# Eight weight transposes moved behind the batches' matrices in the first part of a two-layer attention kernel

## The reference

```
x = x + xattn0(layernorm(x), ctx)          # softmax attention, 16 heads of 32, with biases and temperatures
x = x + ffn0(layernorm(x))                 # relu(quant_linear(x, w1, b1)) -> quant_linear(., w2, b2)
x = x + xattn1(layernorm(x), ctx)          # scores without softmax, then layernorm(q + o)
x = x + tanh(layernormed x through three 512x512 matrices + bias)
# quant_linear rounds the weights per output row: s = max|w| / 127, q = clip(round(w / s), -128, 127)
```

## Time and profile before

| | us |
|---|---|
| median of 3 runs | 2006.84 (2006.36 to 2008.04) |
| the profiled execution's own time | 2011.76 |
| its span | 2010.0 |
| TensorE busy in the span | 1871.1 (93%) |
| VectorE, ScalarE, GpSimd busy | 1583.9, 1232.9, 952.4 |

### The profile page before, as it was taken

One profiled execution on the slowest core, in us unless ns is written; L12 is line 12 of the kernel. 1 busy time (PEld: TensorE's weight loads), 2 busy tenths in 40 slices (PEclk: granted clock), 3 DMA queues, 4 the chain that ended last, 5 costly groups with the idle time before them and its releaser, 6 DMA issues. The chain is left out here.

```text
span 2010.0 us, 30847 instructions
## 1 busy us (share of the span) xinstructions
PE 1871.1 (93%) x9191; PEld 1364.4 (68%) x9274; DVE 1583.9 (79%) x3612; ACT 1232.9 (61%) x3387; POOL 952.4 (47%) x1053
## 2 busy tenths in 40 slices
PE   6698789999999999999986999988999999999997
PEld 5576577877777778777863444446767767767775
DVE  6846578888887888888765888887888888888884
ACT  3434588888787878888862333235655555555543
POOL 2210355555555555555551000025666666666664
PEclk9799799999999999999998999999999999999999
DMA  8346101222223212321117999825445445444310
GB/s 276 122 136 220 48 32 58 71 77 64 64 69 81 64 61 63 78 64 43 42 50 274 391 353 363 317 108 205 147 157 185 156 159 186 159 159 159 139 53 38
DMA packets 124680, 276.03 MB, mean 137 GB/s; under 512 B 41056, under 2 KB 51296, under 8 KB 106208
## 3 DMA queue, kind: packets, MB, share of 16 engines
q1 hardware_dynamic: 121680, 272.69, 39.6%
q10 hardware_dynamic: 2832, 1.32, 0.3%
HBM read 165.95 MB, written 108.00 MB: 136 GB/s over the span
## 5 line engine op out<-in xcount | busy, mean ns | idle before, releaser
L1095 POOL TENSOR_TENSOR a_pr<-a_pr,a_rcp 128x512 f32<-128x512 f32 x256 | 266.5, 1041 | 348.5 <-DVE a_rcp L948 348.5
L871 ACT ACTIVATE a_pr<-a_s,a_nmax 128x128 f32<-128x128 f32 x1024 | 361.6, 368 | 64.4 <-DVE a_nmax L941 62.3
L1322 PE MATMUL f_pair<-f_room,w 128*128 128x512 bf16 x999 | 226.2, 383 | 11.8 <-DVE hmax L1549 9.2
L941 DVE TENSOR_REDUCE a_nmax<-a_s 128x4 f32<-128x512 f32 x256 | 175.6, 686 | 56.7 <-PE a_s L60 52.9
L871 ACT ACTIVATION_READ_ACCUMULATOR a_pr<-a_s,a_nmax 128x1 f32 x1024 | 211.0, 206 | 0.0
L1549 DVE CUSTOM_DVE_ANT_0 f_hf<-f_pair,nb,sh 128x512 f32<-128x512 f32 x248 | 175.0, 748 | 39.7 <-PE f_pair L1322 25.6
L956 DVE TENSOR_TENSOR a_pTl<-a_pt,a_pTh 128x512 fp32r<-128x512 f32 x256 | 175.3, 685 | 37.4 <-ACT a_pTh L880 37.4
L1769 POOL TENSOR_TENSOR f_ring<-f_ring,f_room 128x512 f32<-128x512 f32 x64 | 82.1, 1282 | 256.0 <-DVE f_room L1710 256.0
L1322 PEld LDWEIGHTS f_pair<-f_room,w 128*128 128x128 bf16 x1024 | 99.6, 99 | 126.7 <-DVE hmax L1549 9.7
L880 ACT ACTIVATE a_pTh<-a_pt 128x512 fp32r<-128x512 f32 x256 | 156.0, 609 | 29.9 <-PE a_pt L784 29.9
L784 PE MATMUL a_pt<-ident,a_pr 128*128 128x128 f32 x1024 | 157.2, 276 | 16.4 <-POOL a_pr L1095 8.7
(11 more groups left out here) (398 smaller groups left out, 5245.4 us busy)
## 6 DMA issues: line engine op xcount, KB each, us to landing
hidden<-f_hf SPq DMA_DIRECT2D x58, 1024.0 KB, 7.1
f_hf<-hidden SPq DMA_DIRECT2D x58, 1024.0 KB, 5.2
xb<-x SPq DMA_DIRECT2D x16, 1024.0 KB, 5.4
a_xr<-x SPq DMA_DIRECT2D x64, 256.0 KB, 3.6
x<-a_xr SPq DMA_DIRECT2D x64, 256.0 KB, 2.1
f_ring<-x SPq DMA_DIRECT2D x64, 256.0 KB, 4.8
out<-f_ring SPq DMA_DIRECT2D x64, 256.0 KB, 4.5
f_room<-x SPq DMA_DIRECT2D x15, 1024.0 KB, 9.7
```

The lines of the kernel that those rows point to most:

```text
L871: last = e.activation(pr[:, t, j, :], s_bank[t][:, j * P:j * P + P], ACT.Exp, bias=nmax[kk % 2][:, t, j:j + 1], accum_out=sums[kk % 2][:, ...
L941: e.tensor_reduce(nmax[kk % 2][:, t, :], s_bank[t][:].rearrange("p (j n) -> p j n", j=4), AX, ALU.max, negate=True).then_inc(*e_max)
L1095: e.tensor_tensor(p, p, rcp[kk % 2][:, t, :].unsqueeze(2).to_broadcast([P, 4, KEYS]), ALU.mult).then_inc(*e_pn)
L1322: last = e.matmul(h_bank[(PAIRS * u + i) % 3][:, q, :], w1[:, k, f * P:f * P + P], xT[u % 2][:, k, :], start=k == 0, stop=k == KC - 1)
```

## The change

- The transposes of pieces 0 to 3 leave their places behind `V`, `k1`, `v1` and `bd`. Piece 0 stands behind `bd` of batch 0; the others stand behind `mb` of the batches by the tuple `TURNS`, 1 then 2 then 3 and 4 then 5 and 6; piece 7 stands between `wc` 1 and `wc` 2, with the `row` product.
- VectorE quantises piece 0 behind the third weight, and the others by `PARTS`: 1, then 2 and 3, then 4 and 5, then 6, each ahead of that batch's `mb`; piece 7 behind the four `t`. There are three `qb` tiles.
- The transposes of a piece are two lots of eight into whole banks of 1024 columns, and ScalarE makes two copies instead of four.
- The raw loads come in another order. The eight first chunks are split pairwise (ctx, then weight), and the first product follows them pair by pair. The four bias rows move from ScalarE's queue to SyncE's; the three small vectors are issued by ScalarE behind its eight chunks.
- The centring of Wo1 stands between the second and third evacuation of `k1`; `v1` is evacuated in two pairs around the split of Wq1; in batch 3 the split of A2 stands behind the copies of `m`.

```diff
-        order = [plain("ctxT"), plain("WkT0"), w1_rows(0), plain("WvT0"), plain("WkT1"), w1_rows(1), plain("WvT1"),
-                 w1_rows(2), plain("WoT1"), plain("Wq1"), w1_rows(3), w2_rows(0), w2_rows(1), w2_rows(2), plain("A1T"),
+        order = [plain("ctxT"), plain("WkT0"), plain("WvT0"), plain("WkT1"), w1_rows(0), plain("WvT1"), w1_rows(1),
+                 plain("WoT1"), plain("Wq1"), w1_rows(2), w1_rows(3), w2_rows(0), w2_rows(1), w2_rows(2), plain("A1T"),
                  plain("A2"), w2_rows(3), plain("WT"), plain("WqT0"), plain("WoT0"), x_rows[0], x_rows[1]]
+        TURNS, PARTS = ((1,), (2,), (3, 4), (5, 6)), ((1,), (2, 3), (4, 5), (6,))
...
# TensorE
+                for h in range(2):
+                    e_turned.wait_ge(e, 2 * (q - 1) + h)
+                    for m in (2 * h, 2 * h + 1):
+                        for j in range(4):
+                            at = (m % 2) * D + j * P
+                            last = e.transpose(bankb[h][:, at:at + P], part, identb[:])
...
                 product(place["mb"][b], ...)
+                for q in TURNS[b]:
+                    turn(q)
...
# ScalarE
-            with nc.allow_non_contiguous_dma(reason="few small vectors"):
-                for o, i in small:
-                    e.dma_start(o, i).then_inc(*e_small)
-            chunks(0, ctxT)
-            chunks(1, slot[0])
+            chunks()
+            with nc.allow_non_contiguous_dma(reason="few small vectors"):
+                for o, i in small:
+                    e.dma_start(o, i).then_inc(*e_small)
...
             blocks(0)
-            turned(0, 3)
+            turned(0)
...
# VectorE
             weight(1)
+            quantise(0)
             biased("V", 0, 4)
-            quantise(0, 1)
             weight(2)
-            biased("k1", 1, 8)
-            quantise(0, 2)
+            biased("k1", 1, 8, (0, 1))
             centre(W_LOAD[W_CENTRED])
+            biased("k1", 1, 8, (2, 3))
             weight(3)
+            biased("v1", 2, 12, (0, 1))
             weight(4)
-            biased("v1", 2, 12)
-            quantise(0, 3)
+            biased("v1", 2, 12, (2, 3))
             blocks(0)
-            quantise(1, 0)
...
+                for q in PARTS[b]:
+                    quantise(q)
...
# SyncE
+            load(2)
+            load(3)
+            for i in range(3):
+                bias_row(i)
+            load(4)
+            load(5)
             for c in range(KC):
                 send_k(c)
             load(6)
+            load(7)
             for b in range(NB):
                 send_v(b)
+            bias_row(3)
+            for i in (8, 9, 10, 11):
                 load(i)
             send_m(0)
+            load(12)
+            send_m(1)
+            load(13)
+            load(14)
+            send_m(2)
+            load(15)
+            send_w2(0)
+            load(16)
+            load(17)
+            send_m(3)
+            send_w2(1)
+            send_w2(2)
+            for i in (18, 19, 20, 21):
                 load(i)
+            send_w2(3)
```

More of the change, by code:

```diff
@@ L90, in prepare @@
         bqf = sb("bqf", [P, KC, P])
-        rows = sb("rows", [P, 4, D])
-        qb = [sb(f"qb{i}", [P, 4, D], BF16) for i in range(2)]
+        rows = sb("rows", [P, 3, D])
+        qb = [sb(f"qb{i}", [P, 4, D], BF16) for i in range(3)]
         wst = [sb(f"wst{i}", [P, 4, D], BF16) for i in range(2)]
@@ L136, in prepare @@
         e_first, e_raw = [[ev(f"first{i}{q}", 16) for q in range(KC)] for i in range(2)], [ev(f"raw{i}", 16) for i in range(ring)]
-        e_small = ev("small", 16)
+        e_small, e_rows = ev("small", 16), ev("rows", 16)
         e_zero, e_ident, e_identb, e_ones, e_half, e_diag, e_zeroed = (
@@ L156, in prepare @@
                  (cols[:, 3, :], A["L1_xattn_wq_b"].rearrange("(c p) -> p c", p=P))]
-        for i, n in enumerate(("L0_xattn_bv", "L1_xattn_wk_b", "L1_xattn_wv_b", "L1_xattn_wo_b")):
-            small.append((rows[:, i, :], A[n].rearrange("(a n) -> a n", a=1).to_broadcast([P, D])))
+        ROWS = ("L0_xattn_bv", "L1_xattn_wk_b", "L1_xattn_wv_b", "L1_xattn_wo_b")
+        TURNS, PARTS = ((1,), (2,), (3, 4), (5, 6)), ((1,), (2, 3), (4, 5), (6,))
         block = ctx.enter_context(nc.Block())
@@ L173, in product, with turn @@
                 last.then_inc(*e_prod)
-            def turn(which, i):
-                u = i % 2
-                q = 4 * which + i
+            def turn(q):
+                which, i = divmod(q, 4)
                 e_quant.wait_ge(e, q)
                 e_identb.wait_ge(e, 0)
[L180 to L185, removed]
+                for h in range(2):
+                    e_turned.wait_ge(e, 2 * (q - 1) + h)
+                    for m in (2 * h, 2 * h + 1):
+                        for j in range(4):
+                            part = qb[q % 3][:, m, cut(j)] if which else qb[q % 3][:, j, cut(m)]
+                            at = (m % 2) * D + j * P
+                            last = e.transpose(bankb[h][:, at:at + P], part, identb[:])
                     last.then_inc(*e_turn)
@@ L241, in _ @@
                                         for q in range(KC)])
[L242 to L249, removed]
             e_wlo.wait_ge(e, 7)
@@ L252, in _ @@
             for i in range(KC):
+                if i == 2:
+                    turn(7)
+                    p = place["row"][0]
+                    e_ones.wait_ge(e, 0)
+                    e_dg.wait_ge(e, 0)
+                    e_gone.wait_ge(e, by_dve[p - 6])
+                    for c in range(KC):
+                        last = e.matmul(bank[p % 6][:, cut(c)], ones[:], dg[:, c, :], start=True, stop=True)
+                    last.then_inc(*e_prod)
                 product(place["wc"][i], [([x[:, q, cut(i)] for x in slot[2]], [x[:, q, :] for x in t1]) for q in range(KC)])
@@ L274, in weight, with turned @@
                 e.activation(slot[W_SLOT[j]][0][:], raw[i % ring][:], ACT.Copy).then_inc(*e_whi)
[L276 to L284, removed]
+            def turned(q):
+                which, i = divmod(q, 4)
+                for h in range(2):
+                    e_turn.wait_ge(e, 2 * q + h)
+                    if which and h == 0:
+                        e_wst[i % 2].wait_ge(e, i // 2 - 1)
+                    ms = slice(2 * h, 2 * h + 2)
+                    dst = wst[i % 2][:, ms, :] if which else scr["w1"][:, ms, i * D:(i + 1) * D]
+                    e.activation(dst, bankb[h][:].rearrange("p (m n) -> p m n", m=2), ACT.Copy).then_inc(*e_turned)
             def staged(n, dst):
@@ L317, in _ @@
                 staged(8 + b, k1[0][:, b, :])
-            turned(0, 1)
             weight(3, place["V"][-1])
+            for b in range(2):
+                staged(12 + b, v1[0][:, b, :])
             weight(4, place["k1"][-1])
-            for b in range(NB):
+            for b in range(2, NB):
                 staged(12 + b, v1[0][:, b, :])
-            turned(0, 2)
             blocks(0)
-            turned(0, 3)
+            turned(0)
             for b in range(NB):
@@ L350, in _ @@
                     e.activation(stage[n % 4][:], bank[p % 6][:], ACT.Identity, bias=share[:]).then_inc(*e_copied)
+                if b + 1 == NB:
+                    weight(6, place["t1"][-1])
+                for q in TURNS[b]:
+                    turned(q)
             weight(7, place["mb"][-1])
@@ L378, in centre @@
                 e_raw[i % ring].wait_ge(e, nth(i))
+                e_rows.wait_ge(e, 3)
                 e.tensor_reduce(means[:, 0:KC], r[:], AX, ALU.add)
-                after(e.tensor_reduce(means[:, KC:KC + 1], rows[:, 3, :], AX, ALU.add))
+                after(e.tensor_reduce(means[:, KC:KC + 1], rows[:, 0, :], AX, ALU.add))
                 after(e.tensor_scalar(means[:], means[:], -1.0 / D, None, ALU.mult))
-                e.tensor_scalar(rows[:, 3, :], rows[:, 3, :], means[:, KC:KC + 1], None, ALU.add)
+                e.tensor_scalar(rows[:, 0, :], rows[:, 0, :], means[:, KC:KC + 1], None, ALU.add)
                 for c in range(KC):
@@ L418, in evacuated, with biased @@
                 fn(stage[n % 4][:], bank[p % 6][:]).then_inc(*e_gone)
-            def biased(kind, bias, n):
-                for b in range(NB):
+            def biased(kind, bias, n, bs=range(NB)):
+                e_rows.wait_ge(e, bias)
+                for b in bs:
                     evacuated(kind, b, n + b, lambda o, i: e.tensor_tensor(o, i, rows[:, bias, :], ALU.add))
@@ L489, in _ @@
                 e_centred.wait_ge(e, 0)
-                e.tensor_tensor(stage[n % 4][:], bank[p % 6][:], rows[:, 3, :], ALU.add).then_inc(*e_gone)
+                e.tensor_tensor(stage[n % 4][:], bank[p % 6][:], rows[:, 0, :], ALU.add).then_inc(*e_gone)
             weight(7)
+            for i in range(KC):
+                halve("t", i, 16 + i, [x[:, i, :] for x in t1])
+            quantise(7)
             e_ident.wait_ge(e, 0)
@@ L517, in _ @@
                 if i == 1:
```

(3 more changed lines are left out.)

78 lines of the change are left out of this document (27 added, 51 removed).

## The result

The changed kernel takes 2011.50 us (median of 20 runs, 2009.64 to 2015.83). The kernel before, on the same chip, takes 2006.45 (20 runs). The ratio is 1.0025, 95% interval 1.0018 to 1.0032: slower by some 5 us, where the forecast was 1999.6 with a range of 1993.5 to 2006.5. The profiled execution has a span of 2011.4 us.

What follows compares the result with a forecast made beforehand. Bounds taken: VectorE's list up to the first `m`, PE's period per batch, then the tail's wait for `x`. Terms -7.9 (`x` earlier) and +0.7 (`row` copy) gave -7.2 us: 2006.84 to 1999.6, range 1993.5 to 2006.5.

Steps and rivals of the forecast that it cites:

- the last lands 5.3 later as in the trace: 15.7: Start: three small vectors issued at 9.3 to 10.4, the last landing 5.3 us after issue, at 15.7.
- an added wait of 2.9: Early chain: VectorE's centring waits 2.9 us more for bias row 3, issued behind all sends of `V`, landing at 44.8.
- the first rival: Early chain longer than written: small vectors and bias row 3 at 8.3, adding 3 + 2 us; 2004.6, chance 0.25.
- the first `m` at 78 or later: Sign that the forecast start is wrong; the first `m` product was expected near 72.
- the first `m` of batch 3 later than 146: Sign that the prediction is wrong; batch 3 was forecast to start at 138.8.
- First `m`: 72.4 forecast: End of VectorE's early list: TensorE's first `m` product at 72.4, 23.4 us earlier than before.
- Batch 0: 24.5 forecast: Batch 0 takes 24.5 us, 4.4 more than before, as `mb` waits for `m` 0's send behind three loads.
- the second rival: Batch 0: sends don't stand behind loads, so it takes 19.1 to 20 us; 1994.6, chance 0.12.
- Batches 1 and 2: 20.4 and 21.4 forecast: Batch 1 takes 20.4 us by VectorE's list; batch 2 takes 21.4, its turns sharing two banks with ScalarE's copies between.
- the third rival: Start of batch 1: PE idles and its clock falls to half, costing 8.9 to 14.8 us; 2008.5 to 2014.4, chance 0.11.
- Tail: `x` at 182.3 forecast: Tail: the first `x` group's load, behind piece 7, lands at 182.3, 7.9 us earlier than 190.16.
- The chance of "slower": Whole kernel more than 0.2% slower: 0.08, from a long half-clock dip and the far ends of the first rival.

Runs made afterwards that it cites:

- e5: Changed kernel, with SyncE holding load 3 until the three small vectors have landed: 2006.36 us, ratio 1.0001.
- e1: Changed kernel, with ScalarE issuing the three small vectors ahead of its eight chunks: 2009.69 us, ratio 1.0016.
- e10: Changed kernel with small vectors first and bias row 3 early, sends of m 0 left behind loads 9 to 11: 2001.89 us, ratio 0.9977.
- e3: Changed kernel, with SyncE sending m 0 to 3 of batch 0 ahead of loads 9 to 11: 2004.26 us, ratio 0.9991.
- e6: Changed kernel, with load 20 (first x group) issued ahead of load 19, which waits for piece 7: 2008.51 us, ratio 1.0014.
- e9: Kernel before with the change's new start, small vectors still at the head, and load 20 (x) ahead of load 19: 2000.93 us, ratio 0.9976.
- e8: Kernel before with only the new start (paired chunk splits, bias rows on SyncE behind load 3), small vectors still at the head: 2003.37 us, ratio 0.9990.
- e7: Changed kernel with small vectors first, bias row 3 early, m 0 to 3 ahead of load 9, and x ahead of load 19: 1990.91 us, ratio 0.9931.
- e4: Changed kernel with small vectors first, bias row 3 early, and m 0 to 3 sent ahead of loads 9 to 11: 1995.78 us, ratio 0.9946.
- e2: Changed kernel, with bias row 3 given a free tile and issued with the other three rows: 2006.31 us, ratio 1.0001.

## Why the prediction was wrong

The waits were foreseen where they came, and two terms of the early chain were mis-sized. The failed steps are "the last lands 5.3 later as in the trace: 15.7" (it landed 10.7 later, at 21.6) and "an added wait of 2.9" for bias row 3 (it was 6.1). The first of them also put the first rival aside: "the same vectors landed in 5.3 beside bulk". Two of the prediction's own signs of being wrong came true: the first `m` at 78 or later (82.77), and the first `m` of batch 3 later than 146 (150.44).

- **Small vectors: 15.7 forecast, 21.67 measured (6.0).** Two parts. They go out at 9.80 to 10.91, behind the splits of the chunks, which took until then; and they land 7.2, 9.7 and 10.7 later. The 5.3 of the earlier trace rows is from a vector issued at 1.8, at the head, where the loads were only beginning: the DMAs moved 220 GB/s from 1.8 to 7.1 there, and 301 from 9.8 to 21.6 after. My upper bound of 8.3 was from a 256 KB row and still too low. The same trace held a longer landing, of the next row on that queue, which I didn't take:

```profile
p_rows<-L_xattn_wo_b ACTq DMA_DIRECT2D x1, 256.0 KB, 9.8
```

  e5 shows the traffic to make 10.7 out of 2.4. At the end of the part the wait is worth 4.8 us (e1, where the first product starts 1.0 later) to 6.3 (e5). The Trainium skill, DMA: Bandwidth & Descriptors, section Rules for kernel authors, says that a last dimension that isn't contiguous is split into one descriptor per element, and these vectors are read so. The trace agrees: ScalarE's queue, which carries nothing else in the first 22 us after, shows 1584 packets with 0.01 MB, and three vectors have 1536 elements. That would explain why 2 KB are so sensitive; no run here changed their layout.
- **Bias row 3: 2.9 forecast, 6.1 measured (3.2).** The row took 5.1 for 4.1. The rest is mainly the issue: it waits for the last send of `V`, and GpSimd's fourth half of `V` took 3.35 us where I had put 1.29, from one row:

```profile
45.57 3.35 POOL L542 TENSOR_TENSOR p_outs3l<-p_stage,p_outs3h 128x512 fp32r<-128x512 f32 x1
```

- **First `m`: 72.4 forecast, 82.77 measured.** 6.0 + 3.2 are 9.2 of the 10.4. The other 1.2 are spread over hand-overs and stay open. That no other term was far off is shown by e10: there the rest of the early chain took 1.9 us more than forecast, batch 0 took 0.9 more, and the next two batches took 0.3 and nothing more. Its end agrees to 0.3 us because the 2.9 of row 3 is missing against them, so part of that agreement is luck.
- **Batch 0: 24.5 forecast, 25.3 measured, right.** `mb` 0 waits for a send that stands behind three loads; e3 takes it away and the batch takes 19.4, where the forecast had 19.1. This term was in the forecast, at its price, and it refutes the second rival (sends don't stand behind loads).
- **Batches 1 and 2: 20.4 and 21.4 forecast, 21.0 and 21.35 measured, right.** Around the start of batch 1 the third rival appears in small: TensorE idles 4.94, and the clock falls, with these windows (width, busy time and count on PE, PEld, DVE, ACT, POOL, clock, DMA share, GB/s):

```profile
104.00:106.00 2.00, 0.30 (x1) 0.30 (x2) 1.05 (x2) 0.00 (x0) 0.00 (x0) 0.62 0.98 376
106.00:108.00 2.00, 1.99 (x9) 1.69 (x8) 2.00 (x5) 0.00 (x0) 0.00 (x0) 0.50 0.39 145
...
110.00:112.00 2.00, 2.00 (x8) 1.57 (x7) 1.28 (x4) 0.62 (x2) 0.00 (x0) 0.67 0.00 0
```

  It is at the lower of the two levels, 1.2 GHz, for some 6 us, and not for the 20 of the earlier trace rows; batch 0 is longer than forecast by 0.8 us and batch 1 by 0.6, not by 9. In e3 nothing of the kind happens and batch 1 takes 20.9. This rival is refuted at its price; the prediction's other figure, a loss of about 2 us, is nearer.
- **Tail: `x` at 182.3 forecast, 194.24 measured.** 11.6 of the 11.9 are inherited (first `m` of batch 3 at 150.44, forecast 138.8). The load hangs on piece 7, as forecast. But I left unsaid that it has a price: exchanging the two loads gives 2.6 us (e6 against the changed kernel), 4.1 (e9 against e8) and 4.3 (e7 against e4) in the traces.
- **Sum.** The part ended at 207.06 for 196, which is 11.1 of the miss of 11.9. The rest lies in how the trace's gain was carried over to the median. For the ten edited kernels and the changed one, the median's distance to the kernel before lies 0.4 to 4.0 us (mean 2.3) above the distance of their second parts to 203.03. So the one profiled execution of before may have been about 2 us late in this part; one execution doesn't show it. It matters all the same: e10 reaches the forecast's 196, and its median is 4.3 us below its neighbour's, not 7.2. A right sum for the part would still have left the gain 2.9 us too large.

The first rival (2004.6) had the right mechanism with 5 us where 9 to 10 were lost; with its own bounds it could not reach the slower side. The chance of "slower" stood almost wholly on the clock, a mechanism that did not decide.

Taken together, in the traces' us: against the kernel before, the new start gives 4.2 (e8) and the rest of the change 8.4 (e9 against e7), 12.6 in all. The three waits that the change brought (late small vectors, late bias row 3, sends behind loads) cost 16.4 (e4 against the changed kernel). The place of load 20 is worth nearly the same on both sides (4.1 and 4.3). That leaves a loss of 4, as measured in the traces; the medians have 5. This only divides the difference between the two kernels, in one order of the steps, and is no further test of it.

## What to carry to other kernels

When a large load is moved away from a moment, ask which small transfer moves into its place: a landing time holds only for the traffic in which it was read, so bound a small transfer by the busiest stretch it may fall into, not by its own row in a quieter one. On one queue, put what an engine is waiting for ahead of what only fills buffers: e3 and e6 only exchange the order of issues, and each pays. If a change of several edits comes out near zero, its parts may still be large: here 12.6 us of gain lay under 16.4 of waits, and the version that keeps the gain without the waits (e7, which also loads `x` earlier) is 0.7% faster than the kernel before.

## What the runs showed of the hardware

- The same three 2 KB vectors, issued at the same time, landed in 2.4 to 2.5 us with later loads held back (e5), and in 7.2, 9.7 and 10.7 beside them. Beside the same loads and a fourth row they landed in 2.9, 6.7 and 9.3 (e2): between executions this differs by a us or two. With hardly anything else in flight they still keep the DMA engines busy: from 12.0 to 12.6 in e5 the engines' share is 0.55 while they move 4 GB/s.
- A send of 256 KB behind three loads of 1 MB on SyncE's queue landed 10.3 us after issue, and 2.0 when it went ahead of them (e3).
- TensorE's first products take 0.63 us a matmul for 0.39 later, in the kernel before from 15.28 to 20.96, after from 5.64 to 12.22, in e1 from 6.67 to 14.19: an earlier start is worth less than it looks. 0.63 is what a matmul takes at a granted clock of 0.50 (below, in the dip at the start of batch 1 after), but the profile's clock reads 1.00 in these first stretches, in the earlier trace rows and in the first 16 us after. The prediction's 0.44 us at half clock was read there, from the distances and not from the clock. In e1 VectorE waits for these products (1.53, 2.48, 1.71), the last time when they are already at 0.39. The window of the first 16 us after (columns as above), then one matmul of the dip:

```profile
0.00:16.00 16.00, 9.44 (x28) 6.43 (x29) 5.95 (x13) 8.24 (x10) 1.21 (x10) 1.00 0.88 286
```

```profile
110.81 0.63 PE L58 MATMUL p_bank<-p_ctxTh,p_sloth 128*128 128x512 f32 x1
```

- GpSimd's subtraction of 128x512 took 1.30 us three times and then 3.35 (45.57). The long one is the one beside VectorE's split of 128x2048 (45.28), and that split takes 2.48 where others take 2.28. The same pair stands in every kernel with the changed order (3.34 to 3.37 beside 2.47 to 2.48). That the one slows the other was not tested by taking them apart.
